# A two-layer graph-attention kernel: in layer 1 ACT issues the operand loads and the store of z, SP only the transposes

## The reference, cut to what matters

```python
# x: [8, 2048, 64]; first a small graph layer and a layer norm, then per batch b and head h (4 heads):
h = jnp.einsum('bnc,hdc->bhnd', x, Wh)                 # [8, 4, 2048, 64]
def _gat_layer(h, mask, b):
    scores = jnp.einsum('...nd,...md->...nm', h, h)    # 2048 x 2048 of each (b, h)
    scores = jnp.where(mask, scores, NEG)
    attn = jax.nn.softmax(scores, axis=-1)
    return jnp.einsum('...nm,...md->...nd', attn, h) + b
out_h = _gat_layer(h, mask[None, None], bh[None, :, None, :])
z = jax.nn.leaky_relu(cat(out_h), negative_slope=0.2)
h2 = jnp.einsum('bnk,dk->bnd', z, Wo)
out2 = _gat_layer(h2, mask[None], bo)                  # layer 2: one attention for each batch
# leaky relu, layer norm, residual, layer norm
```

## Time and profile before

| | |
|---|---|
| median of three runs | 3358.05 us (3353.57 to 3359.98) |
| the profiled execution, time | 3353.93 us |
| the profiled execution, span from the first to the last instruction | 3352.2 us |
| layer 1 | about 420 to 2535 us of the span |
| PE, DVE, ACT, POOL busy over the span | 91%, 83%, 70%, 75% |
| mean granted TensorE clock | 0.967 of full speed |
| DMA queue q1 (all that SP issues) | 497.6 MB, 69.9% of 16 engines' span |

### The profile page before, as it was taken

One profiled execution on the slowest core, in us unless ns is written; L12 is line 12 of the kernel. 1 busy time (PEld: TensorE's weight loads), 2 busy tenths in 40 slices (PEclk: granted clock), 3 DMA queues, 4 the chain that ended last, 5 costly groups with the idle time before them and its releaser, 6 DMA issues. The chain is left out here.

```text
span 3352.2 us, 127058 instructions
## 1 busy us (share of the span) xinstructions
PE 3066.7 (91%) x49399; PEld 2295.4 (68%) x49399; DVE 2766.2 (83%) x5392; ACT 2336.7 (70%) x2678; POOL 2507.0 (75%) x1828
## 2 busy tenths in 40 slices
PE   3874599999999999999999999999996699999997
PEld 3433477777777777777777777777765577777775
DVE  5486488888888888888888888888876699999998
ACT  1104577777777777777777777777765588888886
POOL 1023189999999899999999999999986346676776
PEclk7887899999999999999999999999998899999998
DMA  5104879989999998999898899989966533333331
GB/s 205 66 0 150 285 134 164 164 154 170 167 156 161 165 164 157 161 166 161 156 170 166 156 163 167 161 158 174 163 124 209 189 123 125 118 135 119 134 120 73
DMA packets 1189157, 507.55 MB, mean 151 GB/s; under 512 B 1090718, under 2 KB 1148508, under 8 KB 1186588
## 3 DMA queue, kind: packets, MB, share of 16 engines
q1 hardware_dynamic: 1187564, 497.60, 69.9%
q0 software_dynamic: 1200, 3.93, 0.3%
HBM read 102.12 MB, written 62.91 MB: 49 GB/s over the span
## 5 line engine op out<-in xcount | busy, mean ns | idle before, releaser
L605 POOL TENSOR_TENSOR mask_slot<-probs 128x1024 f16<-128x1024 f32 x1024 | 1916.2, 1893 | 221.7 <-ACT probs L962 146.5
L962 ACT ACTIVATE probs<-scores,shifted_max 128x2048 f32<-128x2048 f32 x512 | 1026.1, 2004 | 177.0 <-DVE shifted_max L1165 172.9
L1160 DVE CUSTOM_DVE_ANT_0 scores<-ps,mask 128x1024 f32<-128x1024 f32 x512 | 625.8, 1222 | 206.6 <-PE ps L820 204.7
L819 PE MATMUL ps<-operands 128*128 128x512 f16 x2048 | 778.2, 380 | 12.4 <-DMA v_parts<-h_d 11.3
L820 PE MATMUL ps<-operands 128*128 128x512 f16 x2048 | 777.5, 380 | 0.0
L967 ACT COPY probsT<-ps 128x1024 bf16<-128x1024 bf16 x512 | 518.1, 1012 | 352.3 <-PE ps L828 352.3
L1160 DVE CUSTOM_DVE_ANT_0 scores<-ps,mask,neg_max 128x1024 f32<-128x1024 f32 x512 | 657.4, 1284 | 99.7 <-issue 52.8
L828 PEld LDWEIGHTS ps<-ident,probs 128*128 128x128 bf16 x8192 | 519.6, 98 | 291.9 <-issue 157.6
L828 PE MATMUL ps<-ident,probs 128*128 128x128 bf16 x8192 | 623.7, 219 | 5.8 <-DVE probsT L1169 3.6
L839 PE MATMUL ps<-v_parts,probsT 128*128 128x64 f16 x8192 | 548.0, 193 | 0.0
L838 PE MATMUL ps<-v_parts,probsT 128*128 128x64 f16 x8192 | 547.6, 193 | 0.0
(11 more groups left out here) (169 smaller groups left out, 4545.2 us busy)
## 6 DMA issues: line engine op xcount, KB each, us to landing
mask_slot<-mask SPq DMA_DIRECT2D x129, 512.0 KB, 2.9
operands<-hT_d SPq DMA_DIRECT2D x40, 512.0 KB, 4.2
operands<-hT_d SPq DMA_DIRECT2D x80, 256.0 KB, 4.0
v_parts<-h_d SPq DMA_DIRECT2D x40, 512.0 KB, 4.6
scores<-in_adj SPq DMA_DIRECT2D x16, 1024.0 KB, 4.8
h_d<-probs SPq DMA_DIRECT2D x32, 512.0 KB, 3.5
hT_d<-probs SPq DMA_DIRECT2D x32, 512.0 KB, 2.8
probsT<-mask_slot SPq DMA_TRANSPOSE x1024, 3.5
```

What stands on the lines that cost most here:

```text
L605: pool.tensor_tensor(low[:, u, w], probs[:, u, w], high[:, u, w], ALU.subtract).then_inc(sem(f"low{half}"), 1)
L819: pe.matmul(ps[:, b, :], hi_lo[:, p, t * P:(t + 1) * P], hi_lo[:, p, w], start=True, stop=False)
L962: act.activation(probs[:, 1 - u, :], scores[:, 1 - u, :], ACT.Exp, bias=shifted_max[:, 1 - u:2 - u], scale=-1.0, accum_out=row_sum[:, held ...
L1160: dve.tensor_tensor_reduce(scores[:, u, w], ps[:, 2 * c:2 * c + 2, :].rearrange("p a n -> p (a n)"), mask[:, t * N + c * 2 * BANK:t * N + ...
```

## The change

In layer 1 the five DMAs of an instance that are no transposes move from SP's program to ACT's. `load_part` gets the issuing engine as an argument. ACT issues the four loads at the end of its steps t = 5, 6, 7 and 8 (they stood in SP's steps t = 3 to 6), behind the copy of the high part; the waits for `high_weighed` and `weighed` before the first one move along. The store of z stays at t = 10, at the end of ACT's step. Start and end of layer 1, and layer 2, keep their loads on SP; the last store of z (instance 31) stays on SP too, and the waits for the earlier stores before `load_z(0, 0)` are written for the semaphores' values at that place.

```diff
+        def load_part(eng, i, parity, k):
+
+            s = sem(f"operands{parity}")
+            if k == 3:
+                eng.dma_start(v_parts[:, parity, :], h_d[:, i, :] if isinstance(i, int) else h_d[:, bass.ds(i, 1), :]).then_inc(s, 16)
+                return
+            to, row, at, rows_ = ((hi_lo, 0, 0, P), (lo_hi, 0, D, D), (lo_hi, D, 0, D))[k]
...
@@ SP, layer1_step
                         sp.dma_start_transpose(lowT[:, u, w].rearrange("p (c q) -> p c q", q=P), low[:, u, w]).then_inc(sem(f"low_turned{half}{u}"), 16)
-                k = t - 3
-                if 0 <= k < OPERAND_DMAS and not (isinstance(i, int) and i in (0, LAYER1 - 1, LAYER1)):
-                    if k == 0:
-                        sp.wait_ge(sem("high_weighed"), i * NT)
-                        gate(sp, "sp")
-                        sp.wait_ge(sem("weighed"), i * NT)
-                        gate(sp, "sp")
-                    load_part(i + 1, 1 - p, k)
-                if t == 10 and not (isinstance(i, int) and i == 0):
-                    store_z(i - 1, 1 - p)
@@ SP, after layer 1
-            for b in range(4):
-                sp.wait_ge(sem(f"z_stored{b % 2}"), 16 * (b // 2 + 1))
+            for u in range(2):
+                sp.wait_ge(sem(f"z_stored{u}"), 8 * LAYER1 - 16 * u)
             load_z(0, 0)
-            store_z(LAYER1 - 1, 1)
+            sp.wait_ge(sem("out_copied"), LAYER1 * 4)
+            sp.dma_start(z_d[:, LAYER1 - 1, :], outs[:, 1, :]).then_inc(sem("z_stored1"), 16)
@@ ACT, layer1_step
                     act.copy(highT[:, u, N // 2:N], high_bank(1)).then_inc(sem("high_copied1"), 1)
+                k = t - 5
+                if 0 <= k < OPERAND_DMAS and not (isinstance(i, int) and i in (0, LAYER1 - 1, LAYER1)):
+                    if k == 0:
+                        act.wait_ge(sem("high_weighed"), i * NT)
+                        gate(act, "act")
+                        act.wait_ge(sem("weighed"), i * NT)
+                        gate(act, "act")
+                    load_part(act, i + 1, 1 - p, k)
+                if t == 10 and not (isinstance(i, int) and i == 0):
+                    act.wait_ge(sem("out_copied"), i * 4)
+                    gate(act, "act")
+                    act.dma_start(z_d[:, i - 1, :] if isinstance(i, int) else z_d[:, bass.ds(i - 1, 1), :],
+                                  outs[:, 1 - p, :]).then_inc(sem(f"z_stored{1 - p}"), 16)
```

More of the change, by code:

```diff
@@ L367, in finish @@
             assert last or len(steps) == FINISH_STEPS
+        def load_part(eng, i, parity, k):
[4 more added lines that the diff above has]
+            to, row, at, rows_ = ((hi_lo, 0, 0, P), (lo_hi, 0, D, D), (lo_hi, D, 0, D))[k]
+            at = i * P + at
+            eng.dma_start(to[row:row + rows_, parity, :],
+                         hT_d[at:at + rows_, :] if isinstance(i, int) else hT_d[bass.ds(at, rows_), :]).then_inc(s, 16)
         @block.sync
@@ L417, in _ @@
                 sp.wait_ge(sem(f"hT_stored{u}"), 8 * UNITS)
[L419 to L428, removed]
             for i in range(2):
                 for k in range(OPERAND_DMAS):
-                    load_part(i, i, k)
+                    load_part(sp, i, i, k)
             def step(g, u, instance, t, parity, tile):
@@ L448, in step @@
                         gate(sp, "sp")
-                    load_part(instance + 1, 1 - parity, k)
+                    load_part(sp, instance + 1, 1 - parity, k)
             def more(instance):
                 return not isinstance(instance, int) or instance not in (0, LAYER1 - 1, LAYER1, INSTANCES - 1)
-            def store_z(i, p):
-                sp.wait_ge(sem("out_copied"), i * 4 + 4)
-                gate(sp, "sp")
-                sp.dma_start(z_d[:, i, :] if isinstance(i, int) else z_d[:, bass.ds(i, 1), :], outs[:, p, :]).then_inc(sem(f"z_stored{p}"), 16)
             def layer1_step(g, i, t, p, back):
@@ L529, in _ @@
                 for k in range(OPERAND_DMAS):
-                    load_part(LAYER1 + i, i, k)
+                    load_part(sp, LAYER1 + i, i, k)
             store_h2T(B - 1, 1)
```

## The result

The changed kernel took 3373.37 us (median of 7 runs, 3369.18 to 3385.94), the kernel before 3358.05 (7 runs, 3351.93 to 3359.98): a ratio of 1.0056 [1.004, 1.0072]. The forecast was 3353.3. The time lies within the stated range of 3347 to 3378, but only because the range reached up to most of rival 3: the mechanism of the sum did not come, that of rival 3 did, at about six tenths of its price.

A forecast was written before the change was run, and what follows sets the result against it. PE was taken as the bound, so only its waits could be saved: -5.7 us for loads leaving SP plus 1.0 for ACT's issues gave -4.7, from 3358.05 to 3353.3 us; range 3347 to 3378.

The forecast's parts named there:

- rival 3: Transposes in flight: loads from another queue disturb them more, PE loses about 0.8 us a load; +24 us, 3382; chance 0.15.
- the sum: Whole kernel: -5.7 + 1.0 = -4.7 us, giving 3353.3 us from the median of 3358.05.
- PE is the bound, and only its waits matter: Loop of layer 1: PE busy 2000.69 of 2010 us, so a DMA matters only through PE's waits.
- At most 8.5 us to gain: Loop of layer 1: all disturbances cost 7.4 us over 26 instances with loads, 8.5 us over 30; the ceiling.
- ACT's issues, +1.0 us: ACT, five issues an instance: hidden beside the copy with 1.17 us of cover; +1.0 us, between 0 and 11.
- The removal, -5.7 us: SP's queue: loads no longer delay transposes, ending most PE waits; two thirds of 8.5 us saved, bounds 0 and -8.5.
- the 0.6 us of SP: SP's queue: delay a load's issue puts on the next transpose, about 0.6 us a load, counted as gone.
- the 0.83 to 1.66 us: DMA engines: time a 256 KB or 512 KB load takes of all 16, whoever issues it, counted as staying.
- Rival 1: Loads' work on the DMA engines delays transposes, SP's saving is absorbed, waits only move: 3358, within 2; chance 0.22.
- The tests that I named: Trace signs; wrong on the DMA engines if PE's L811 waits stay at 6 us or grow, landings above 6.8.

The follow-up runs named there:

- e6: The kernel before without layer 1's operand loads from instance 2 on (PE reuses operands of instances 0 and 1), z still on SP: 3348.1 us.
- e12b: The changed kernel with six semaphore increments ahead of each ACT DMA, loads at t = 5, 7, 9, 11 and z at t = 14: 3345.4 us.
- e2: The kernel before with SP issuing the loads two steps later, t = 5 to 8, z still at t = 10: slower by 0.11%.
- e3: The changed kernel with ACT issuing the loads two steps earlier, t = 3 to 6, z still at t = 10: 3382.1 us.
- e8b: The kernel before, all on SP, with loads at t = 3, 5, 7, 9 and z at t = 12, a repeat: 3353.1 us.
- e1: The kernel before with SP issuing each load and the store of z between a tile's two transposes, still one queue: 3399.0 us.
- e7: The kernel before with only the store of z issued by ACT, behind its copy at t = 10, loads left on SP: 3366.7 us.

## The prediction against this, step by step

- **PE is the bound, and only its waits matter**: right. The loop's +22.5 us is PE's +23.5 us at that one line.
- **At most 8.5 us to gain**: right in size; e6 found 9.2. Only e12b's medians go beyond it, by 11.4 us against before on the same chip, and its loop does not: 1700.8 us for 13 turns against the 1695.7 of undisturbed ones.
- **ACT's issues, +1.0 us**: the cover held. All 151 read 0.33 to 0.55 us and start inside the copy (1506.66 in a copy from 1506.50 to 1507.51), and the exponential keeps its idle time of 0.28 us from DVE. They start 0.02 to 0.34 us behind the copy's start, 95 of them within the 0.2 us named. No run shows the +1.0 by itself, and nothing is left for it: PE's waits for transposes cover the loop's loss. The Trainium skill, "Perfetto Trace Analysis", section "DMA Instruction — HWDGE (DVE, Sync)", would have had them up to 1.8 us long, by the estimate that the prediction made from its lock. The trace does not agree: at 1506.66 SP was in the middle of a transpose's issue and ACT's row is 0.49 us.
- **A reading of the rows.** The prediction has the transpose "behind the load" at 2.71 us. Rows 7 are the second transpose of that pair; the pair's first, directly behind the load, began only 1.36 us earlier (1484.97). Already there a load lengthened a second half's issue.
- **The removal, -5.7 us: the step that failed.** It was priced as "the 0.6 us of SP as gone and the 0.83 to 1.66 us as staying", and "hit other tiles there" was the only place considered. That other tiles are hit is harmless (e2, e3). What I did not ask is at which *moment of a tile* ACT issues, and which of the two halves the load then meets. The earlier trace rows gave the first half of the answer: ACT's DMA is issued at the copy's start. SP's timeline would have given the other: in before as in after, a second half's issue begins some 0.3 to 0.7 us before the copy of that step (medians by tile), and so, in after, mostly 0.65 to 1.05 us before ACT's load; it lasts 1.24 us. The load's own work stays the same, as I wrote, but it moves from the half with 2.2 to 4.5 us to spare to the one with 1.2 to 2.8. What came in place of -5.7 us was PE's wait for transposes rising from 5.9 to 29.4 us. Whether the 0.6 us of SP was ever worth anything no run shows: with the moment mended, e12b's medians beat e8b's by 7.7 us, but their loops are equal (1700.8 and 1701.0 us).
- **Rival 3** named the mechanism, from a single instruction packet in the earlier trace rows, and gave it 0.15. It had no timeline of the two queues; that the time fell inside the range is owed to this rival, not to the sum. Its threshold of 0.9 us of added delay was passed: `v_parts`, where it came in the middle of an issue, added 2.1 to 5.2 us to a landing of 2.75. It charged 0.8 us to each of 30 instances, +24; the medians differ by 15.3, 0.51 us each. It thought of the load and the transpose as sharing the engines; in the packets of after, `v_parts` passes the transpose's end almost whole in 13 of 26 instances and hardly at all in the other 13. Rows 14 deserved more weight: they were the only rows that showed what a second queue does to a transpose.
- **Rival 1**, with the rule of the Trainium skill, "DMA: Bandwidth & Descriptors", section "Issuing engines are not separate DMA queues": that the transfers interleave is what happened (q10's packets run among q1's). That only issue time is saved by a second engine holds for the gain; the loss is not in it. The moment at which they meet was worth 26 us.
- **The tests that I named** worked: waits at PE's line above 6 us, and landings above 6.8 us. In after the longest is 9.3:

```profile
L465 SPq DMA_TRANSPOSE probsT<-mask_slot x972: 1231/1233/3783, 429.4 to 2439.0; - x195
...
DMA to landing us min/median/max: 2.7/3.6/9.3
```

The median, 3.6, is that of the earlier trace rows: a median over a thousand transposes hides this altogether.

What stays open: where the medians of e12b gain on those of e8b, since their loops are equal; and why e12b (3345.4) comes out about as fast as e6 (3348.1), which has no loads at all. In the traces it does not: 13 turns took 1700.8 us in e12b and 1695.5 in e6, and the spans are 3350.0 and 3345.5 us. The two ran on different chips, and in e6 z is still at t = 10 in SP's queue. What decides in the hardware whether a load passes the end of a transpose was not looked into.

## What to carry to other kernels

A queue of one's own takes away the order that a shared queue gave for nothing. Before moving a DMA to another engine, find the moment of the period at which that engine will issue it, and which transfer of the critical chain is being issued or is in flight then; prefer the start of the gap behind the transfer with the least time to spare, and look again at those instances in which something else (here an instruction fetch) holds that transfer up. Semaphores that enforce the place can cost more than they save, where the waiting engine has work queued behind; a few instructions of delay, in cover that is there anyway, did it here for nothing, but hold only as long as the kernel's rhythm does.

## What the runs showed of the hardware

- A DMA of another queue gets ahead of a transpose that is still being issued. SP takes 1.24 us to issue one; a 512 KB load 0.64 to 0.81 us into that makes it land after 4.9 to 8.0 us, one at 1.02 to 1.17 us leaves it at 2.7 to 3.0 (after, `v_parts`). In the first case 106 to 128 of the load's 128 packets start before the transpose's last ones, in the second 5 to 15. If a fetch holds the transpose up, the later load passes it too: at 1.14 to 1.23 us, 5.2 to 5.5 in 10 of 11 instances (e12b, tile 9).
- A transpose alone lands after 2.75 us. One during which the instruction queue fetches takes 3.8 to 3.95 on average (e6: means 2.74 to 2.76 without a fetch, 3.79 to 3.93 with, 313 and 440 transposes; before and after agree). With a 512 KB load (z) just ahead and no fetch it takes 3.55 (e1, tile 8's second half, 12 times), with both 5.62 (14 times).
- For the same store z and with a fetch too, a second half fared nearly alike with either queue: 5.62 us in e1 (SP, just ahead of it) and 5.58 in after (ACT, within its issue). Without a fetch there are only 3.55 in e1 and 4.37 in e7 (ACT, 4 times), and the moments differ, so the queue's own share is not isolated.
- ACT's and SP's issues run side by side without a visible wait for each other; ACT's 151 rows in after last 0.33 to 0.55 us; only one of 31 issues of z in e7 was long, 2.69 us.
